# Seven PSUM banks for PE's sums in the third edge pass, and VectorE's additions placed later behind them

## The chip, the cores and the metric

The kernel runs on one core of one Trainium2 chip. The metric is the device time of one execution in microseconds (us). The kernel before took 9835.41 us, the median of three runs that lay between 9833.75 and 9841.89 us. PE is TensorE, DVE is VectorE, ACT is ScalarE, POOL is GpSimd and SP is SyncE, which issues plain DMAs.

## The reference, cut to what matters

Four graph layers follow each other over 6250 nodes and 100000 edges, each with a residual and a layer norm. The second is the one that the change is in. It has two attention heads of 128 columns:

```python
def _gat_head(node_feats, W, a, src, dst, N):
    h = node_feats @ W
    a_l, a_r = (a[0, :C], a[0, C:])
    s_l = h @ a_l
    s_r = h @ a_r
    logits = s_l[src] + s_r[dst]
    e = jnp.exp(-jax.nn.leaky_relu(logits, negative_slope=ALPHA))
    row_sum = jax.ops.segment_sum(e, src, num_segments=N)
    h_prime = jax.ops.segment_sum(e[:, None] * h[dst], src, num_segments=N)
    return jax.nn.elu(h_prime / row_sum[:, None])
```

For each edge, a row of `h` is fetched by `dst`, multiplied by the edge's weight `e`, and added to the sum of its node `src`. `e` itself is one more column, so that a row has 2 x (128 + 1) = 258 columns. No maximum is subtracted in this layer, unlike in the first and the third.

## The kernel before

The edges are sorted by the node whose sum they enter, once by `dst` and once by `src`, and cut into 832 chunks of 128 edges. All edges of a chunk belong to one window of 128 nodes. Six edge passes go over the 832 chunks: a1e and a2e (the two attention layers of the first graph layer), **be** (the layer above), te (dot product attention), and g1e and g2e (plain sums). The first four are `attention_pass`, with `kind` "gat", "gat", "neg" and "dot"; the last two are `sum_pass`. `guarded` is true for "gat" and "dot", so the branches with `not guarded` are of be alone. Between the passes lie dense stages. A pass begins and ends with a barrier of all engines.

A pass is unrolled in 104 steps of eight chunks. Each engine has its own written order, and the engines meet by semaphores alone. In be, with t the step:

- POOL (`gather`) issues eight indirect DMAs a step. Each fetches the 128 rows of a chunk from the table in HBM into a ring of four steps (`RING`). Before the even chunks it waits for DVE's `weigh` of the step four before, which frees the slots.
- SP (`fetch`) loads `place_row`, the place of each edge in its window.
- DVE (`turn`) makes from it the one-hot matrix `turned`, two steps ahead, and PE (`of_node`) multiplies it with `node`, which gives each edge its node's term. DVE adds the three parts of that (`sum_parts`), adds the fetched row's term (`meet`, which first waits until all eight gathers of step t have landed) and applies the leaky slope (`leak`).
- ACT (`weights`) makes the exponentials of a step and (`distances`, `mark`) the one-hot matrix of the next.
- DVE (`weigh`, four times a step, two chunks each, L1239) multiplies the rows with their weights.
- PE (`sums`, eight times a step, L1077) multiplies the one-hot matrix of a chunk with its 258 columns, into a PSUM bank, `ps_u`. Four banks are used in turn.
- DVE (`add`, eight times a step, L1251) adds the bank to the window's part of `acc` in SBUF. The window's number comes from a register, that `Windows` loads for four steps at a time; the first chunk of which it holds a number is the argument `-12`, counted from the step's own.

Semaphores count: `s_summed` PE's sums, `s_added` DVE's additions, `s_summand` the `weigh`s. A sum waits until the addition that empties its bank is done, four chunks before, and an addition waits for its own sum and for the addition before it. In DVE's step t the rows of step t-1 are weighed, the additions 4 to 7 of step t-2 are made, and then the additions 0 to 3 of step t-1.

## Time and profile before

| what | value |
|---|---|
| device time, median of three runs | 9835.41 us |
| device time, lowest and highest | 9833.75, 9841.89 us |
| span of the profiled execution | 11006.2 us |
| pass be in the profiled execution, first gather to last addition | 5247.3 to 6562.2 us |
| DVE, PE and POOL busy in that stretch | 661.5, 721.7 and 812.0 us |
| granted TensorE clock: whole span, that stretch | 0.695, 0.70 |

The profiled execution's own time is known by its span alone, 11006.2 us from the first to the last instruction. It is 1170.8 us, or 12%, above the median of the timed runs, which are executions without the profiler. A number of the trace therefore has to be asked whether it also holds in a timed run. In the rows further down, "idle before" is the time for which an engine did nothing ahead of an instruction, and the name behind it is what ended most of it: "issue" means nothing that the profile shows, "remote" a semaphore whose last event fits no instruction recorded next to it. The shape of an operand is partitions x elements.

### The profile page before, as it was taken

What the parts mean: (1) busy time and instruction counts of PE and PEld (TensorE: products, weight loads), DVE (VectorE), ACT (ScalarE), POOL (GpSimd) and SP (SyncE); (2) the same over time, 40 slices, a digit from 0 to 9 for tenths busy, and PEclk for the clock granted to TensorE, in tenths of its full rate; (3) what the DMA queues carried; (4) which work ended last, traced back from release to release, by engine and by line L of the source; (5) the groups of instructions that cost most, each with busy time, mean ns of one, the idle gap of its engine ahead of it and who ended that gap; (6) DMA issues with size and microseconds to landing.
All of it is one profiled execution on the core that took longest, in us unless ns stands there. A gap on an engine that the chain in (4) does not pass through costs nothing. (4 is left out here: it accounts for less than half of the span.)

```text
span 11006.2 us, 145249 instructions
## 1 busy us (share of the span) xinstructions
PE 6188.8 (56%) x34036; PEld 4327.9 (39%) x34036; DVE 6265.2 (57%) x19166; ACT 4406.9 (40%) x12341; POOL 6558.0 (60%) x6616
## 2 busy tenths in 40 slices
PE   3774577566666444446455557778775343433335
PEld 2443344333343444444233334445554232333334
DVE  7998899566666433335455557999984121211113
ACT  7886788222222222223222223444443233333333
POOL 4996699355554455552566642666655666566663
PEclk6997799766666555556667779999987555555556
DMA  0222122233333212212333343666652111211112
GB/s 21 74 74 67 45 73 73 87 98 99 96 98 82 62 41 41 42 41 45 105 106 107 108 93 123 175 175 175 174 159 64 46 47 45 41 27 23 23 23 35
DMA packets 464040, 862.04 MB, mean 78 GB/s; under 512 B 143184, under 2 KB 204036, under 8 KB 463108
## 3 DMA queue, kind: packets, MB, share of 16 engines
q0 software_dynamic: 226304, 550.69, 20.8%
q1 hardware_dynamic: 236932, 302.17, 9.4%
q8 instruction: 316, 5.18, 0.2%
q14 instruction: 488, 4.00, 0.1%
HBM read 800.28 MB, written 52.14 MB: 77 GB/s over the span
## 5 line engine op out<-in xcount | busy, mean ns | idle before, releaser
L1031 POOL DMA_INDIRECT all_Y<-table,all_row x3328 | 3236.2, 972 | 2394.2 <-DVE all_Y L1239 1243.1
L557 POOL TENSOR_SCALAR all_acc<-all_Y,all_acc 128x128 f16<-128x128 f16 x1176 | 1319.0, 1133 | 229.3 <-DVE all_acc L492 158.9
L1239 DVE TENSOR_TENSOR all_Y<-all_Y 128x512 f32<-128x512 f32 (+1 forms) x1560 | 942.5, 604 | 187.3 <-issue 100.3
L1466 POOL DMA_INDIRECT g2e_rows<-table,all_row x832 | 784.9, 943 | 432.3 <-issue 234.7
L1466 POOL DMA_INDIRECT g1e_rows<-table,all_row x832 | 785.1, 944 | 419.4 <-issue 234.3
L1077 PE MATMUL be_ps_u<-all_Y,be_onehot 128*128 128x258 f32 x1664 | 645.7, 523 | 546.5 <-DVE all_acc L1251 281.8
L1482 PE MATMUL g1e_ps_u<-g1e_rows,g1e_onehot 128*128 128x128 f32 x1664 | 470.3, 426 | 737.0 <-issue 557.9
L1482 PE MATMUL g2e_ps_u<-g2e_rows,g2e_onehot 128*128 128x64 f32 x1664 | 434.8, 431 | 771.9 <-issue 549.5
L1510 DVE TENSOR_TENSOR all_acc<-all_acc,g1e_ps_u 128x128 f32 x832 | 240.0, 288 | 968.0 <-DMA te_place_row<-places_src 594.5
L1077 PE MATMUL a1e_ps_u<-all_Y,a1e_onehot 128*128 128x264 f32 x1664 | 762.3, 589 | 20.1 <-DVE all_acc L1251 11.1
L1510 DVE TENSOR_TENSOR all_acc<-all_acc,g2e_ps_u 128x64 f32 x832 | 184.5, 222 | 1026.1 <-DMA te_place_row<-places_src 624.0
L1482 PEld LDWEIGHTS g2e_ps_u<-g2e_rows,g2e_onehot 128*128 128x128 f32 x1664 | 382.0, 321 | 824.8 <-issue 632.5
L1251 DVE TENSOR_TENSOR all_acc<-all_acc,be_ps_u 128x258 f32 x832 | 350.5, 421 | 606.2 <-remote 385.7
L1482 PEld LDWEIGHTS g1e_ps_u<-g1e_rows,g1e_onehot 128*128 128x128 f32 x1664 | 359.5, 275 | 847.8 <-issue 679.8
L1077 PEld LDWEIGHTS be_ps_u<-all_Y,be_onehot 128*128 128x128 f32 x1664 | 370.7, 253 | 768.5 <-issue 675.4
L495 DVE TENSOR_SCALAR all_acc<-all_Y,all_acc 128x832 f16<-128x832 f16 x1568 | 599.5, 442 | 0.0
L1063 PE MATMUL te_ps_q<-all_X,te_turned 128*128 x1664 | 515.3, 440 | 146.8 <-issue 103.6
L1077 PE MATMUL te_ps_u<-all_Y,te_onehot 128*128 128x264 f32 x1664 | 532.2, 435 | 73.6 <-DVE all_Y L1239 71.5
L1077 PE MATMUL a2e_ps_u<-all_Y,a2e_onehot 128*128 128x66 f32 x1664 | 492.1, 434 | 124.9 <-issue 86.9
L524 ACT ACTIVATE all_Y<-all_Y 128x128 f16<-128x128 f16 x1568 | 476.7, 388 | 96.4 <-PEq L81 96.4
L532 ACT ACTIVATE all_Y<-all_Y,all_acc 128x128 f16<-128x128 f16 x1568 | 477.1, 389 | 3.0 <-DMA all_Y<-codes 3.0
L1077 PEld LDWEIGHTS a2e_ps_u<-all_Y,a2e_onehot 128*128 128x128 f32 x1664 | 397.8, 318 | 145.8 <-issue 121.5
(521 smaller groups left out, 15166.9 us busy)
## 6 DMA issues: line engine op xcount, KB each, us to landing
all_Y<-table,all_row POOLq DMA_INDIRECT x3328
all_Y<-lows SPq DMA_DIRECT2D x196, 256.0 KB
all_Y<-codes SPq DMA_DIRECT2D x196, 256.0 KB
a1e_place_row<-places_dst SPq DMA_DIRECT2D x104, 256.0 KB
a2e_place_row<-places_dst SPq DMA_DIRECT2D x104, 256.0 KB
be_place_row<-places_src SPq DMA_DIRECT2D x104, 256.0 KB
te_place_row<-places_src SPq DMA_DIRECT2D x104, 256.0 KB
te_flags<-flags_src SPq DMA_DIRECT2D x832, 6.0 KB
```

Source lines behind the costliest of these rows:

```text
L495: dve.tensor_scalar(column1[b][:, k, :], lane16, column[b][:, k:k + 1], None, ALU.is_equal).then_inc(s_hot, 1)
L524: act.activation(away[:, k, :], lane16[:, 0:P], ACT.Abs, scale=-1.0, bias=low_t[:, u * 8 + k:u * 8 + k + 1]).then_inc(s_away, 1)
L532: act.activation(unlike[b][:, k, :], code_row[b][:, k * P:(k + 1) * P], ACT.Abs, scale=-1024.0, bias=spaced_t[:, u * 8 + k:u * 8 + k + 1]) ...
L557: pool.tensor_scalar(row1[b][:, k, :], lane16[:, 0:P], row[b][:, k:k + 1], other_t[:, t * 8 + k:t * 8 + k + 1], ALU.is_equal, ALU.mult).th ...
L1031: pool.indirect_dma_start(out=rows[:, r, k, :], out_offset=None, in_=table, in_offset=bass.IndirectOffsetOnAxis(ap=order.row[:, t * 8 + k: ...
L1063: last = pe.matmul(ps_q[pair % 2][:, j * HC:(j + 1) * HC], turned[b][:, k * P:(k + 1) * P], queries[:, bass.ds(windows.at(windows_j, chunk ...
L1077: pe.matmul(ps_u[k % 4][:, 0:R], onehot[b][:, k, :], summand[:, b, k, :], start=True, stop=True).then_inc(s_summed, 1)
L1239: dve.tensor_tensor(out[:, :, :, 0:C], rows[:, r, ks, value_c0:value_c0 + HC].rearrange("p k (h n) -> p k h n", h=H), bc(out[:, :, :, C:C ...
L1251: dve.tensor_tensor(mine, mine, ps_u[k % 4][:, 0:R], ALU.add).then_inc(s_added, 1)
L1466: pool.indirect_dma_start(out=rows[:, r, k, :], out_offset=None, in_=table, in_offset=bass.IndirectOffsetOnAxis(ap=order.row[:, t * 8 + k: ...
L1482: pe.matmul(ps_u[k][:, 0:width], onehot[b][:, k, :], rows[:, r, k, :], start=True, stop=True).then_inc(s_summed, 1)
L1510: dve.tensor_tensor(mine, mine, ps_u[k][:, 0:width], ALU.add).then_inc(s_added, 1)
```

## The change

In be the number of banks goes from four to seven (with the bank of `of_node` these are all eight), and the banks go round by the count of chunks instead of by the chunk's number in its step. A sum then waits for the addition seven chunks before. DVE gets an order of its own for be: its step t makes the additions 2 to 7 of step t-2 and the additions 0 and 1 of step t-1, where it was 4 to 7 and 0 to 3. `sum_parts`, `weigh`, `meet`, `leak` and `turn` are there as often as before; the fourth `weigh` moves ahead of the addition 7 of step t-2. The windows' numbers are loaded from chunk -14 instead of -12, as many as before. The code of the other passes is written in another way, with the same order.

```diff
+    BANKS = 4 if guarded else 7
...
-        ps_u = [m.ps(f"ps_u{b}", [P, 512]) for b in range(4)]
+        ps_u = [m.ps(f"ps_u{b}", [P, 512]) for b in range(BANKS)]
...
-                    wait(pe, s_added, t * 8 + (k - 3))
-                    pe.matmul(ps_u[k % 4][:, 0:R], onehot[b][:, k, :], summand[:, b, k, :], start=True, stop=True).then_inc(s_summed, 1)
+                    wait(pe, s_added, t * 8 + (k + 1 - BANKS))
+                    pe.matmul(ps_u[(t * 8 + k) % BANKS][:, 0:R], onehot[b][:, k, :], summand[:, b, k, :], start=True, stop=True).then_inc(s_summed, 1)
...
-                windows = Windows(nc, order, mybir.EngineType.DVE, -12, U)
+                windows = Windows(nc, order, mybir.EngineType.DVE, -12 if guarded else -14, U)
...
-                    dve.tensor_tensor(mine, mine, ps_u[k % 4][:, 0:R], ALU.add).then_inc(s_added, 1)
+                    dve.tensor_tensor(mine, mine, ps_u[(t * 8 + k) % BANKS][:, 0:R], ALU.add).then_inc(s_added, 1)
...
+                    elif not gat:
+                        sum_parts(t, b)
+                        add(t - 2, 2, -14, j)
+                        weigh(t - 1, n, rp, 0)
+                        add(t - 2, 3, -13, j)
+                        meet(t, b, r)
+                        add(t - 2, 4, -12, j)
+                        weigh(t - 1, n, rp, 1)
+                        leak(t, b)
+                        add(t - 2, 5, -11, j)
+                        weigh(t - 1, n, rp, 2)
+                        add(t - 2, 6, -10, j)
+                        weigh(t - 1, n, rp, 3)
+                        add(t - 2, 7, -9, j)
+                        add(t - 1, 0, -8, j)
+                        turn(t + 2, b)
+                        add(t - 1, 1, -7, j)
+                        return
```

The order on PE, ACT, POOL and SP is the one of before. On DVE the first half of a step of be stands here, of before and of after. `be_spread` is written by `sum_parts`, `all_Y` by `weigh`, `all_acc` by `add` (the row "ISA" ahead of it computes its address and carries the wait for the sum), `be_raw` by `meet` and `be_argument` by `leak`. Before:

```order
L1264 TENSOR_REDUCE be_spread1<-be_ps_n 128x16
L1239 TENSOR_TENSOR all_Y<-all_Y 128x4x128
L1251 ISA
L1251 TENSOR_TENSOR all_acc<-all_acc,be_ps_u0 128x258
L1270 TENSOR_TENSOR be_raw<-be_spread1,all_Y 128x16
L1251 ISA
L1251 TENSOR_TENSOR all_acc<-all_acc,be_ps_u1 128x258
L1239 TENSOR_TENSOR all_Y<-all_Y 128x4x128
L1278 SCALAR_TENSOR_TENSOR be_argument1<-be_raw 128x16
```

After:

```order
L1265 TENSOR_REDUCE be_spread1<-be_ps_n 128x16
L1252 ISA
L1252 TENSOR_TENSOR all_acc<-all_acc,be_ps_u6 128x258
L1240 TENSOR_TENSOR all_Y<-all_Y 128x4x128
L1252 ISA
L1252 TENSOR_TENSOR all_acc<-all_acc,be_ps_u0 128x258
L1271 TENSOR_TENSOR be_raw<-be_spread1,all_Y 128x16
L1252 ISA
L1252 TENSOR_TENSOR all_acc<-all_acc,be_ps_u1 128x258
L1240 TENSOR_TENSOR all_Y<-all_Y 128x4x128
L1279 SCALAR_TENSOR_TENSOR be_argument1<-be_raw 128x16
```

One addition more now stands ahead of the first `weigh` and ahead of `meet`, and each is of a chunk two earlier. The end of the same step, from the third `weigh` on, before:

```order
L1239 TENSOR_TENSOR all_Y<-all_Y 128x4x128
L1251 ISA
L1251 TENSOR_TENSOR all_acc<-all_acc,be_ps_u0 128x258
L1239 TENSOR_TENSOR all_Y<-all_Y 128x4x128
L1251 ISA
L1251 TENSOR_TENSOR all_acc<-all_acc,be_ps_u1 128x258
L1251 ISA
L1251 TENSOR_TENSOR all_acc<-all_acc,be_ps_u2 128x258
L1251 ISA
L1251 TENSOR_TENSOR all_acc<-all_acc,be_ps_u3 128x258
L1229 TENSOR_SCALAR be_turned1<-be_place_row1,all_lane_p 128x1024
```

After:

```order
L1240 TENSOR_TENSOR all_Y<-all_Y 128x4x128
L1252 ISA
L1252 TENSOR_TENSOR all_acc<-all_acc,be_ps_u3 128x258
L1240 TENSOR_TENSOR all_Y<-all_Y 128x4x128
L1252 ISA
L1252 TENSOR_TENSOR all_acc<-all_acc,be_ps_u4 128x258
L1252 ISA
L1252 TENSOR_TENSOR all_acc<-all_acc,be_ps_u5 128x258
L1230 TENSOR_SCALAR be_turned1<-be_place_row1,all_lane_p 128x1024
L1252 ISA
L1252 TENSOR_TENSOR all_acc<-all_acc,be_ps_u6 128x258
```

Before, the first addition behind the third `weigh` is of the sum of this step's first rows; after, it is the addition 6 of the step before, and the first addition of this step's sums stands behind the fourth `weigh` and the addition 7. `turn` is followed by one more addition.

## Rows read from the trace of the kernel before

**Rows 1.** The page's first line.

```profile
span 11006.2 us, 145249 instructions
```

**Rows 2.** Busy time of each engine by pass: a1e, a2e, be, te, g1e, g2e.

```profile
core 0: us, PE busy (x) PEld busy (x) DVE busy (x) ACT busy (x) POOL busy (x), PEclk, DMA share, GB/s
2067.00:3545.00 1478.00, 921.27 (x3906) 575.98 (x3906) 938.04 (x2785) 404.14 (x1239) 836.44 (x832) 0.66 0.38 97
3680.00:5090.00 1410.00, 663.61 (x3952) 569.79 (x3952) 553.08 (x2824) 402.72 (x1248) 792.64 (x832) 0.50 0.24 46
5246.00:6563.00 1317.00, 721.74 (x2496) 442.54 (x2496) 661.53 (x1665) 374.38 (x1040) 812.01 (x832) 0.70 0.40 105
6781.00:8238.00 1457.00, 1123.18 (x4742) 753.29 (x4742) 1316.92 (x2887) 677.68 (x1558) 907.14 (x935) 0.92 0.61 173
8404.00:9618.00 1214.00, 475.44 (x1696) 364.57 (x1696) 245.90 (x842) 367.11 (x942) 785.06 (x832) 0.58 0.20 45
9652.00:10868.00 1216.00, 438.19 (x1681) 384.70 (x1681) 188.61 (x845) 364.08 (x936) 787.88 (x833) 0.50 0.15 23
```

**Rows 3.** The gathers of a1e, a2e, be, g1e, g2e: duration in ns, first and last start.

```profile
L1031 POOL DMA_INDIRECT all_Y<-table,all_row x832: 940/946/1571, 2072.4 to 3525.1; - x167
...
L1031 POOL DMA_INDIRECT all_Y<-table,all_row x832: 938/944/1218, 3683.4 to 5058.9; - x167
...
L1031 POOL DMA_INDIRECT all_Y<-table,all_row x832: 940/946/1464, 5247.3 to 6532.8; - x167
...
L1466 POOL DMA_INDIRECT g1e_rows<-table,all_row x832: 938/944/1045, 8406.6 to 9597.6; - x167
...
L1466 POOL DMA_INDIRECT g2e_rows<-table,all_row x832: 938/944/992, 9656.9 to 10845.9; - x167
```

**Rows 4.** Groups of be by line: busy us, mean ns | idle before, releasers.

```profile
L1031 POOL DMA_INDIRECT all_Y<-table,all_row x832 | 812.0, 976 | 492.6 <-issue 251.6 <-DVE all_Y L1239 223.0 <-POOLq L81 18.0
L1077 PE MATMUL be_ps_u<-all_Y,be_onehot 128*128 128x258 f32 x1664 | 645.7, 523 | 546.5 <-DVE all_acc L1251 281.8 <-issue 263.4
...
L1251 DVE TENSOR_TENSOR all_acc<-all_acc,be_ps_u 128x258 f32 x832 | 350.5, 421 | 606.2 <-remote 385.7 <-PE be_ps_u L1077 115.8 <-issue 75.5
L1239 DVE TENSOR_TENSOR all_Y<-all_Y 128x512 f32<-128x512 f32 x416 | 284.8, 685 | 1.8 <-PE be_ps_u L1077 1.8
```

**Rows 5.** DVE in order of time, be: start us, length us, [idle before].

```profile
5704.39 0.53 DVE L1229 TENSOR_SCALAR be_turned<-be_place_row,all_lane_p 128x1024 bf16<-128x1024 f16 x1
...
5711.36 0.51 DVE L1229 TENSOR_SCALAR be_turned<-be_place_row,all_lane_p 128x1024 bf16<-128x1024 f16 x1
...
5714.79 0.42 DVE L1251 TENSOR_TENSOR all_acc<-all_acc,be_ps_u 128x258 f32 x1 [0.21 <-issue]
5715.13 0.69 DVE L1239 TENSOR_TENSOR all_Y<-all_Y 128x512 f32<-128x512 f32 x1
5724.26 0.42 DVE L1251 TENSOR_TENSOR all_acc<-all_acc,be_ps_u 128x258 f32 x1 [8.44 <-remote]
...
5727.97 0.55 DVE L1229 TENSOR_SCALAR be_turned<-be_place_row,all_lane_p 128x1024 bf16<-128x1024 f16 x1
...
5736.41 0.48 DVE L1229 TENSOR_SCALAR be_turned<-be_place_row,all_lane_p 128x1024 bf16<-128x1024 f16 x1
```

**Rows 6.** PE in order of time, the same stretch.

```profile
5713.25 1.13 PE L1077 MATMUL be_ps_u<-all_Y,be_onehot 128*128 128x258 f32 x4
5714.72 1.31 PE L1077 MATMUL be_ps_u<-all_Y,be_onehot 128*128 128x258 f32 x4 [0.35 <-issue]
5724.83 1.20 PE L1077 MATMUL be_ps_u<-all_Y,be_onehot 128*128 128x258 f32 x2 [8.80 <-issue]
```

**Rows 7.** POOL in order of time, the same stretch.

```profile
5715.28 1.35 POOL L1031 DMA_INDIRECT all_Y<-table,all_row  x1 [0.30 <-issue]
...
5723.19 0.95 POOL L1031 DMA_INDIRECT all_Y<-table,all_row  x1 [0.30 <-issue]
5726.07 0.95 POOL L1031 DMA_INDIRECT all_Y<-table,all_row  x1 [1.93 <-DVE all_Y L1239]
```

More of the change, by code:

```diff
@@ L1381, in step @@
                         return
+                    elif not gat:
[16 more added lines that the diff above has]
+                        return
                     else:
-                        if t == 0 or not gat:
+                        if t == 0:
                             sum_parts(t, b)
@@ L1395, in step @@
                     weigh(t - 1, n, rp, 2)
-                    if guarded:
-                        scan_forward(t, b)
-                        fade_first(t - 1, n, -8, j)
-                        scan_back(t, b)
-                        add(t - 1, 0, -8, j)
-                        weigh(t - 1, n, rp, 3)
-                        row_scan_forward(t, b)
-                        add(t - 1, 1, -7, j)
-                        row_scan_back(t, b)
-                        add(t - 1, 2, -6, j)
-                        drop(t, b)
-                        turn(t + 2, b)
-                        add(t - 1, 3, -5, j)
-                        widen(t, b)
-                        top(t, b)
-                        if gat:
-                            sum_parts(t + 1, n)
-                        subtract(t, b)
-                    else:
-                        add(t - 1, 0, -8, j)
-                        weigh(t - 1, n, rp, 3)
-                        add(t - 1, 1, -7, j)
-                        add(t - 1, 2, -6, j)
-                        add(t - 1, 3, -5, j)
-                        turn(t + 2, b)
+                    scan_forward(t, b)
+                    fade_first(t - 1, n, -8, j)
+                    scan_back(t, b)
+                    add(t - 1, 0, -8, j)
+                    weigh(t - 1, n, rp, 3)
+                    row_scan_forward(t, b)
+                    add(t - 1, 1, -7, j)
+                    row_scan_back(t, b)
+                    add(t - 1, 2, -6, j)
+                    drop(t, b)
+                    turn(t + 2, b)
+                    add(t - 1, 3, -5, j)
+                    widen(t, b)
+                    top(t, b)
+                    sum_parts(t + 1, n)
+                    subtract(t, b)
                 if guarded:
```

## The prediction

> **What bounds the kernel now.** I read the page's first line, then the busy time by pass, then the gathers of each pass, then the groups of be and three engines of it in order of time.
>
> The first line is the oddest: the profiled execution spans 11006.2 us [rows 1], 1170.8 more than the timed median of 9835.4. So the first question is not what be waits for in the trace, but whether a timed run waits for it too.
>
> In be no engine is full: of 1317 us DVE is busy 661.5, PE 721.7 and POOL 812.0 [rows 2]. Three paces can be read.
> - POOL: a gather takes 0.976 us [rows 4], and where nothing holds it the next starts 0.30 us later [rows 7]. That is 1.276 us each and 8 x 1.276 = **10.2 us a step**. 832 of them take 1062 us, but first to last start is 6532.8 - 5247.3 = 1285.5 us [rows 3]. The difference, 224 us, is the wait for DVE's `weigh` to free slots (223.0 us [rows 4]).
> - DVE and PE together: from one `turn` to the next are 6.97 us (5704.39 to 5711.36) and 8.44 us (5727.97 to 5736.41) [rows 5]. Both are below POOL's 10.2.
> - Between these two lies a step of 16.6 us. In it DVE sits idle 8.44 us, put down to "remote" [rows 5], ahead of the addition of a sum that PE's rows show as issued at 5713.25 [rows 6]. PE records four sums until 5716.0, and then nothing for 8.80 us, since the fifth needs DVE's addition. So PE's work is there and its semaphore is late. Such waits sum to 385.7 us [rows 4], as many as 46 of 8.4 us in 104 steps, so nearly every second step has one.
>
> So in the profiled execution be alternates a quick step and one with a silence of PE, and DVE then frees slots too late for POOL. A timed run without the silences would be bound by POOL alone.
>
> **Are the silences in a timed run?** I test it on the whole kernel. If POOL ran at its pace in every pass whose gathers are held up, each would shrink from its first-to-last time to its busy time plus 832 x 0.30 = 249.6 us [rows 2, 3]: a1e from 1452.7 to 1086.0, a2e from 1375.5 to 1042.2, be from 1285.5 to 1061.6, g1e from 1191.0 to 1034.7, g2e from 1189.0 to about 1037. In te, DVE is busy 1316.9 of 1457 us, and I leave it. The differences are 367 + 333 + 224 + 156 + 152 = **1232 us**, against the 1171 us by which the trace is longer than the median. The two agree to 61 us. If the silences were in the timed runs as well, 1171 us would have to be found elsewhere, and te, where DVE is busy 90% of the time, has no room for them. I therefore take it that a timed run has them hardly at all, and that be takes POOL's pace there.
>
> The Trainium skill (page "NOTIFIC — the notification-queue block", section "Interfaces") says of the path by which records leave the engines that its backpressure "is what can stall an engine". That would make the silences the profiler's own. No row here shows that path; by that rule the result is the forecast below, and no number of it rests on it.
>
> **The change part by part.**
> - *Seven banks.* PE's sum waits for the addition seven chunks back. In the trace PE waits 281.8 us for additions [rows 4]. In a timed run at 10.2 us a step, DVE and PE need 7.0 to 8.4, so they have 1.8 to 3.2 us of slack in each step, and the wait is paid out of that. Worth on the end: 0.
> - *DVE's new order.* Eight additions, four `weigh`s, and one each of `sum_parts`, `meet`, `leak` and `turn`, as before. An addition right behind an addition starts 0.63 us after it (0.42 and 0.21 idle), a `weigh` behind an addition 0.34 us [rows 5]. Three pairs of additions stood together in a step, now one: 2 x 0.29 = 0.58 us of DVE a step, 60 us in all. It is covered by POOL's pace, and comes to light only where DVE is the bound.
> - *What is queued behind the waits.* `meet` waits for the landing of step t's gathers. One addition more stands ahead of it, 0.6 us at most, and behind it stand the other `weigh`s of step t-1. These free the slots for the gathers of step t+3, and POOL is then at t+1: two steps, 20 us, of room. Cost 0. `turn` is two steps ahead of its use, and the fourth `weigh` comes 0.3 to 1 us sooner. Cost 0.
> - *The tail.* The last gather starts at 6532.8 [rows 3]. Behind it DVE must still make its part of step 103 and all of 104 and 105. Before that were 7 + 8 + 4 additions, now 6 + 8 + 6: one more, +0.6 us.
> - *Registers and code.* As many window numbers are loaded as before. 0.
> - *What is left of the waits.* The 61 us by which the reconstruction overshoots may be waits that timed runs do have. By its part of 1232 us, be has 61 x 224 / 1232 = 11 us of them. At most all 61 lie in be. If the change removes two fifths of them (91 of 224, as worked out in the first rival), the gain is 4 to 5 us, with bounds 0 and 61.
>
> Sum: +0.6 - 4.5 = -4 us, so the timed median goes from 9835 to **9831 us**. I make it against the timed median, since the profiled span holds the silences. In the profiled execution itself the change may show more: be could lose up to 224 us of its 1317 there.
>
> **The rivals.**
> 1. *The silences are in the timed runs too, and be is bound by DVE and PE* (faster). Then DVE's order counts. The 60 us of separated additions come through. Under each silence DVE makes one `weigh` more before it blocks, since the first addition of the new sums now stands behind the fourth `weigh`: 0.6 us in each of 52 pairs of steps, 31 us. Together 91 us: 9835 - 91 = **9744 us**. Bounds: 0 (the silence grows by what DVE works ahead) and POOL's pace, 224 us: 9611 us. For it: 385.7 us of DVE's idle time and 223.0 of POOL's in be. Against it: the sum of 1232 against 1171.
> 2. *The gathers grow longer* (slower). A gather takes 976 ns in be and 785.06 / 832 = 944 ns in g1e, where DVE has no `weigh` [rows 2, 4]; the gather at 5715.28, beside a `weigh` at 5715.13, took 1.35 us [rows 5, 7]. So the `weigh`s cost POOL some 32 x 832 = 27 us. If the new order puts twice as many beside gathers, POOL, the bound, pays 27 us more: **9862 us**. It decides from a mean gather of 1000 ns on (24 x 832 = 20 us). Against it: neither the number of `weigh`s nor their length changes.
>    The Trainium skill ("SBUF — State Buffer", section "Who interferes with whom") says that a VectorE instruction with two SBUF inputs contends with a GpSimd instruction that reads SBUF. The 1.35 us fits it. The rule speaks against any change that moves `weigh`s onto gathers; it gives no price here.
> 3. *PE is not set free.* The sum 7 of a step still needs the addition 0 of the same step, at the end of DVE's step, so that PE stays tied to DVE. That too gives no change: 9835 us. I count it with the forecast.
>
> **How the numbers follow.** A measurement of this kernel tells 0.2%, about 20 us, from no change. The forecast, with rival 3, has 0.64. Faster has 0.29: most of it is rival 1, and the rest is the case that most of the 61 us lie in be and go. Slower has 0.07, rival 2. The low end of the range takes in rival 1 at its own price and leaves the stretch from 9740 down to 9611 (about 0.08) out. The high end takes in rival 2. So 9740 to 9860; the forecast's own range is 9815 to 9850.
>
> **What would show each step right or wrong.** In the profile of the changed kernel I expect fewer waits of PE for additions (281.8 before), one pair of additions side by side in a step instead of three, and a quick step of about 6.4 instead of 7.0 us, while a step's eight gathers stay at 10.2 us. The silences should still be there, since nothing in the change touches their cause, and be may shorten in the profile without the timed median moving. That split is the sign of the forecast. The mean gather should stay at 976 ns. The prediction is wrong if the timed median falls by more than 20 us: then be is bound by DVE and PE in timed runs as well, and the step that failed is the test on the whole kernel, with the 1171 us lying elsewhere than in the waits of POOL.

## The result: slower by 22 us, and the profile after

The changed kernel takes 9858.01 us (median of 14 runs, 9850.68 to 9863.64), the kernel before 9835.76 us in as many runs beside it (9828.03 to 9846.62). The ratio is 1.002, with an interval of 1.0013 to 1.0027. So the change costs 22 us where -4 was forecast. The time lies in the range, the sign was given a chance of 0.07, and what made it slower is none of the rivals as they were written.

**Two levels.** One thing has to be known before the numbers can be compared: one and the same program takes some 9830 us in some measurements and some 11020 to 11130 us in others, with or without a profile, and runs that are compared stand beside each other at one level. I call them the lower and the upper level. The profile of the kernel before (11006.2 us, [rows 1]) is an execution at the upper one, the profile of the changed kernel one at the lower. No profile of the kernel before fell at the lower level. Nearest to it there is the run r14_banks_only further down, the kernel before with seven banks, at 1.0004 of its time.

The page's first line, the busy time of be (columns as in [rows 2]) and the gathers of a1e, a2e, be, g1e and g2e (as [rows 3]), of the changed kernel:

```profile
span 9857.9 us, 145246 instructions
```

```profile
4575.00:5710.00 1135.00, 679.95 (x2496) 498.74 (x2496) 659.74 (x1674) 375.80 (x1042) 837.38 (x832) 0.73 0.48 122
```

```profile
L1032 POOL DMA_INDIRECT all_Y<-table,all_row x832: 942/946/1454, 2077.3 to 3186.9; - x167
...
L1032 POOL DMA_INDIRECT all_Y<-table,all_row x832: 940/944/1254, 3336.4 to 4393.3; - x167
...
L1032 POOL DMA_INDIRECT all_Y<-table,all_row x832: 942/946/1475, 4582.2 to 5671.7; - x167
...
L1476 POOL DMA_INDIRECT g1e_rows<-table,all_row x832: 940/944/1045, 7559.6 to 8597.0; - x167
L1476 POOL DMA_INDIRECT g2e_rows<-table,all_row x832: 940/944/992, 8660.7 to 9698.0; - x167
```

The groups of be by line (as [rows 4]):

```profile
L1032 POOL DMA_INDIRECT all_Y<-table,all_row x832 | 837.4, 1006 | 272.5 <-issue 238.8 <-POOLq L81 19.4 <-DVE all_Y L1240 14.3
...
L1078 PE MATMUL be_ps_u<-all_Y,be_onehot 128*128 128x258 f32 x1664 | 611.7, 533 | 268.9 <-DVE all_Y L1240 267.0 <-DVE all_acc L1252 1.8
...
L1252 DVE TENSOR_TENSOR all_acc<-all_acc,be_ps_u 128x258 f32 x832 | 348.7, 419 | 43.2 <-DVE all_acc L1252 16.6 <-PE be_ps_u L1078 8.9 <-issue 7.8
L1240 DVE TENSOR_TENSOR all_Y<-all_Y 128x512 f32<-128x512 f32 x416 | 285.0, 685 | 0.0
```

What the reader is to see: DVE's 385.7 us of silences ("remote", [rows 4]) are gone, and nearly all of POOL's 223.0 us of waits for `weigh` (14.3 are left). POOL idles 272.5 us for 832 gathers, 0.33 each. It is the bound of be, with hardly a hole. PE no longer waits for additions (1.8 us). All this is the level and not the change: r14_banks_only, which has DVE's old order and lies at the lower level, shows the same (POOL waits 19.5 us for `weigh`). But the gathers take 837.4 us instead of 812.0, 1006 ns each instead of 976.

There is one thing more, which no group of be shows, since a register load isn't counted as busy. These are the loads of window numbers (`Windows`, L888) in be: duration in ns (least, median, most), first and last start. Here are DVE's in the kernel before, and then PE's own and DVE's in the changed kernel:

```profile
L888 DVEq TENSOR_LOAD <-all_window x27: 2098/2102/2109, 5264.8 to 6551.1; - x27
```

```profile
L888 PEldq TENSOR_LOAD <-all_window x27: 2127/2134/2152, 4581.6 to 5637.5; - x27
L888 DVEq TENSOR_LOAD <-all_window x27: 7125/7137/7175, 4599.8 to 5689.7; - x27
```

As many numbers are loaded, 27 times 32, but each of DVE's loads takes 7.14 us instead of 2.10. That is 27 x 5.03 = 136 us of DVE's time. In DVE's own order of time one such load looks like this (the idle time in brackets; the load itself has no row):

```profile
5637.91 0.40 DVE L1252 TENSOR_TENSOR all_acc<-all_acc,be_ps_u 128x258 f32 x1
5644.78 0.21 DVE L1265 TENSOR_REDUCE be_spread<-be_ps_n 128x16 f32<-128x48 f32 x1 [6.47 <-issue]
5645.35 0.42 DVE L1252 TENSOR_TENSOR all_acc<-all_acc,be_ps_u 128x258 f32 x1 [0.36 <-issue]
5645.69 0.69 DVE L1240 TENSOR_TENSOR all_Y<-all_Y 128x512 f32<-128x512 f32 x1
5646.29 0.42 DVE L1252 TENSOR_TENSOR all_acc<-all_acc,be_ps_u 128x258 f32 x1
5646.62 0.18 DVE L1271 TENSOR_TENSOR be_raw<-be_spread,all_Y 128x16 f32<-128x16 f32 x1
```

### The profile page after: what moved, and what is told of

It reads as the page before. It is cut to its first block and busy times, and to the rows that moved or that the text cites. A ratio compares the mean times of both kernels' runs of the same rounds, so it can differ in the third digit from the quotient of the medians.

```text
span 9857.9 us, 145246 instructions
## 1 busy us (share of the span) xinstructions
PE 6075.9 (62%) x34036; PEld 4356.6 (44%) x34036; DVE 6264.1 (64%) x19166; ACT 4401.9 (45%) x12341; POOL 6604.6 (67%) x6616
## 5 line engine op out<-in xcount | busy, mean ns | idle before, releaser
L1032 POOL DMA_INDIRECT all_Y<-table,all_row x3328 | 3284.8, 987 | 1497.4 <-issue 1036.6
L1492 PE MATMUL g1e_ps_u<-g1e_rows,g1e_onehot 128*128 128x128 f32 x1664 | 428.7, 439 | 630.8 <-issue 313.7
L1492 PE MATMUL g2e_ps_u<-g2e_rows,g2e_onehot 128*128 128x64 f32 x1664 | 406.5, 426 | 652.3 <-DMA g2e_rows<-table,all_row 327.3
L1078 PE MATMUL be_ps_u<-all_Y,be_onehot 128*128 128x258 f32 x1664 | 611.7, 533 | 268.9 <-DVE all_Y L1240 267.0
L1078 PEld LDWEIGHTS be_ps_u<-all_Y,be_onehot 128*128 128x128 f32 x1664 | 430.8, 272 | 403.5 <-DVE all_Y L1240 312.9
L1064 PEld LDWEIGHTS te_ps_q<-all_X,te_turned 128*128 128x128 f32 x1664 | 320.0, 207 | 299.2 <-issue 258.9
```

Source lines behind the costliest of these rows:

```text
L1032: pool.indirect_dma_start(out=rows[:, r, k, :], out_offset=None, in_=table, in_offset=bass.IndirectOffsetOnAxis(ap=order.row[:, t * 8 + k: ...
L1064: last = pe.matmul(ps_q[pair % 2][:, j * HC:(j + 1) * HC], turned[b][:, k * P:(k + 1) * P], queries[:, bass.ds(windows.at(windows_j, chunk ...
L1078: pe.matmul(ps_u[(t * 8 + k) % BANKS][:, 0:R], onehot[b][:, k, :], summand[:, b, k, :], start=True, stop=True).then_inc(s_summed, 1)
L1492: pe.matmul(ps_u[k][:, 0:width], onehot[b][:, k, :], rows[:, r, k, :], start=True, stop=True).then_inc(s_summed, 1)
```

## The experiments

The first twelve runs test what I first held to be open: whether banks, order or the second SBUF input of `weigh` count. Ten of them fell at the upper level, where the changed kernel itself never ran. r13_after and r14_banks_only repeat two of them at the lower level. r15 to r17 test the load, and r18_after_again is the changed kernel once more. Ratios are this kernel over the kernel before on the same chip, with the 95% interval.

**Both kernels again.** The kernel before once more:

> The kernel before, unchanged, once more with a profile, since the profiled execution shown first spans 11006 us against a timed 9836. Theory A (be is bound by POOL's gathers in a timed run, and the change made them longer): the span is about 9835 us, POOL in be hardly waits for VectorE (under 40 us), the 832 gathers take about 1065 us from first to last start, with a mean near 976 ns, some 30 ns under the 1006 ns of the changed kernel. Theory B (the 22 us come from somewhere else): the mean gather in be is within 5 ns of 1006.

Measured: 11010.6 us, beside 11019.59 as the median of timed runs without a profile. The same once more, on another chip:

> The kernel before, unchanged, with a profile. If this chip is at the lower level (about 9830 us): theory A (the gathers of be, which are the bound, got longer) wants a mean gather in be some 25 to 30 ns under the 1006 ns of the changed kernel, first to last gather about 1065 us against 1090, and the other passes alike within 5 us. Theory B wants the same length of be, and the 20 us in another pass.

Measured: 11157.82 us beside 11130.49. So the timed runs have the upper level as well, and neither run fell at the level that its theories were written for. The changed kernel, three times:

> The changed kernel, unchanged, beside the kernel before on the same chip. The kernel before has shown two levels that have nothing to do with its code: 9836 us, and 11006 to 11020 us with long silences of PE's semaphores. Theory A1: at the upper level be waits on VectorE and PE, and the new order, which lets VectorE weigh two chunks more under a silence, shortens be by up to 91 us (about 10930 beside 11020); at the lower level it is 22 us longer (9858 beside 9836). Theory A2: at the upper level too the new order lengthens be, since VectorE's order is now tied to PE one step later; the run with five banks and the new order was 237 us longer there.

> The changed kernel unchanged. Chips have shown two levels for the same program (9825 to 9836, or 11019 to 11130 us for the kernel before), and the changed kernel has been timed on the lower alone. At the upper level: if VectorE's new order is what made the runs with five banks and weights from PSUM 222 to 252 us longer, this is about 11240, with 220 us more in be; if the five banks or the weights in PSUM were, it is 11020 or less. At the lower level: ratio 1.002, mean gather in be 1006 ns.

> The changed kernel unchanged, once more, for a chip at the upper level. There, with VectorE and PE the bound in be, its loads of 7.13 us put 27 x 5.03 = 136 us more on VectorE's path, less what the new order saves: ratio 1.005 to 1.02. At the lower level: 1.0018 to 1.0020, as three times before.

Measured: 9843.43 against 9825.05 us, 1.0018 (1.0008 to 1.0027); 9847.16 against 9827.51, 1.0018 (1.0009 to 1.0028); 9856.66 against 9834.86, 1.0019 (1.001 to 1.0028). be's gathers stretch over 1090.6, 1090.5 and 1092.5 us from the first one's start to the last one's end, 1090.5 in the profile above, and each of the 27 loads took 7.13 us in all three. The loss is real, and the slow load with it. The chip is not what sets the level: the same one gave the upper level in r1_before_again and the lower in r18_after_again.

**Seven banks alone, in the old order.** DVE's order and the start of its windows stay as before:

```diff
+    BANKS = 4 if guarded else 7
...
-        ps_u = [m.ps(f"ps_u{b}", [P, 512]) for b in range(4)]
+        ps_u = [m.ps(f"ps_u{b}", [P, 512]) for b in range(BANKS)]
...
-                    wait(pe, s_added, t * 8 + (k - 3))
-                    pe.matmul(ps_u[k % 4][:, 0:R], onehot[b][:, k, :], summand[:, b, k, :], start=True, stop=True).then_inc(s_summed, 1)
+                    wait(pe, s_added, t * 8 + (k + 1 - BANKS))
+                    pe.matmul(ps_u[(t * 8 + k) % BANKS][:, 0:R], onehot[b][:, k, :], summand[:, b, k, :], start=True, stop=True).then_inc(s_summed, 1)
...
-                    dve.tensor_tensor(mine, mine, ps_u[k % 4][:, 0:R], ALU.add).then_inc(s_added, 1)
+                    dve.tensor_tensor(mine, mine, ps_u[(t * 8 + k) % BANKS][:, 0:R], ALU.add).then_inc(s_added, 1)
```

> The kernel before with the seven banks and the bank counting of the change, but VectorE's old order. Theory A (the weighings of the new order fall on gathers more often): VectorE's order is to blame and not the banks, so this is the time of before, 9836 us within 5, gathers in be as long as before. Theory B (PE, freed by more banks, slows the gathers or the landing by its own accesses): the 22 us appear here, about 9858 us.

> Seven banks with VectorE's old order, again, since the first run of it was at the upper level, where POOL is not the bound. At the lower level theory A wants the time of before (ratio 1.000) and its mean gather; theory B, that PE's freer running costs the 20 us, wants a ratio of 1.002.

> Seven banks with VectorE's old order, for the lower level (about 9830 us for the kernel before); both runs of it so far fell on chips at the upper level. At the lower level theory A (the new order puts weighings on gathers) wants the time of before, ratio 1.000 within 0.001, and a mean gather in be near 980 ns, against 1006 ns in the changed kernel. Theory B (PE's freer running costs the 20 us) wants 1.002 and 1006 ns. At the upper level: 1.001 to 1.004 as twice before.

> Seven banks with VectorE's old order. At the lower level theory A (the new order puts weighings on gathers) wants the time of before, ratio 1.000 within 0.001, and a mean gather in be near 980 ns against 1006; theory B (PE's freer running costs the 20 us) wants 1.002 and 1006 ns. At the upper level: 1.001 to 1.004, as three times before.

Measured at the upper level: 11039.4 against 11019.59 us, 1.0013 (1.0001 to 1.0024); 11168.31 against 11130.49, 1.0036 (1.0023 to 1.0049); 11032.58 against 11019.29, 1.0014 (1.0005 to 1.0023). At the lower: 9832.45 against 9827.51, 1.0004 (0.9995 to 1.0014). Seven banks gain nothing at either level, and lose a little at the upper one. The lower run stood beside r13_after on one chip, and there the whole change costs 1.0018. So the loss lies in the order or in what came with it. Its span, its gathers, its group of gathers and its loads:

```profile
span 9838.7 us, 145246 instructions
```

```profile
L1032 POOL DMA_INDIRECT all_Y<-table,all_row x832: 942/946/1466, 4581.5 to 5664.9; - x167
```

```profile
L1032 POOL DMA_INDIRECT all_Y<-table,all_row x832 | 831.2, 999 | 272.3 <-issue 233.6 <-DVE all_Y L1240 19.5 <-POOLq L81 19.2
```

```profile
L888 DVEq TENSOR_LOAD <-all_window x27: 2098/2103/2118, 4598.8 to 5681.8; - x27
```

The old order at the lower level has gathers of 999 ns. This is the figure that the 1006 of the changed kernel must be held against, not the 976 of the upper level: where POOL waits less, more of its gathers meet a `weigh` (452 here, 391 in the trace of before). Against this run r13_after's gathers take 6 us more in all, and its last addition ends 6 us later behind the last gather (32.9 and 27.1 us). That is 12 of the 15 us between the two medians.

**Five banks instead of seven in the changed kernel** (`BANKS = 4 if guarded else 5`):

> The changed kernel with five banks in place of seven, nothing else. At the lower level (9836 for the kernel before) POOL is the bound and five banks are enough: 9858, as the changed kernel. At the upper level (11020): if the 237 us of the run with the weights in PSUM and five banks came from the banks, this is about 11256; if they came from VectorE's order, the changed kernel itself is that long, and this too; if they came from the weights in PSUM, this is at 11020 or under it.

Measured: 9846.3 against 9825.05 us, 1.002 (1.0011 to 1.003), with the changed kernel itself at 1.0018 on that chip. In the new order at the lower level it doesn't matter whether there are five banks or seven.

**`weigh` reads its factors from PSUM.** ACT writes `exp` a second time, into two PSUM banks, and `weigh` takes its factors there, so that it has one SBUF input instead of two. The changed kernel has five banks here, to make room:

```diff
+    NWEIGHT = 1 if dot else 2
...
+                ps_w = [m.ps(f"ps_w{b}", [P, 512]) for b in range(2)]
...
+        def factor(b):
+            return ps_w[b][:, 0:8 * H].rearrange("p (h k) -> p h k", h=H)
...
+                        act.activation(factor(b), argument[b][:, 0, :, :], ACT.Exp, scale=-1.0).then_inc(s_weight, 1)
...
-                        dve.wait_ge(s_weight, (t + 1) * NARG)
+                        dve.wait_ge(s_weight, (t + 1) * NWEIGHT)
...
+                    by = out[:, :, :, C:C + 1] if guarded else factor(b).rearrange("p h (k n) -> p k h n", n=1)[:, ks, :, :]
...
-                                      bc(out[:, :, :, C:C + 1], [P, 2, H, C]), ALU.mult).then_inc(s_summand, 1)
+                                      bc(by, [P, 2, H, C]), ALU.mult).then_inc(s_summand, 1)
```

In the kernel before:

> The kernel before, where ScalarE writes be's weights a second time into PSUM (one activation more a step) and VectorE's weighing reads the weight from there, so that it has one input in SBUF in place of two. Theory A (a weighing with two SBUF inputs holds up the gather beside it): mean gather in be falls from about 976 to about 945 to 950 ns, and the time falls by 22 to 27 us to about 9811 us. Theory B (the gathers are slowed by something else, or not at all by the weighing's inputs): mean gather and time as before, 9836 us or a little more.

> The kernel before with the weights of be read from PSUM, again, for the lower level. At the upper level the mean gather in be fell from 974 to 952 ns. Theory A wants that here too, and now in the time: 832 x 22 ns = 18 to 20 us under the kernel before, ratio 0.998. Theory B: ratio 1.000.

In the changed kernel:

> The changed kernel with the same weights from PSUM; the two banks for them are taken from the sums, which have five in place of seven. Theory A: mean gather in be falls from 1006 to about 945 to 950 ns, the order of VectorE no longer matters, and the time is that of the kernel before with weights from PSUM, about 9811 us, 47 below the changed kernel. Theory B: about 9858 us, as the changed kernel.

> The changed kernel with the weights from PSUM and five banks, again, for the lower level, where five banks alone left the changed kernel as it was (ratio 1.002 and 1.0018). Theory A: mean gather in be falls from 1006 to about 952 ns, 832 x 54 = 45 us, so that the ratio to before is about 0.998, the same as that of the kernel before with weights from PSUM. Theory B: ratio 1.002.

> The changed kernel with the weights of be read from PSUM and five banks, for the lower level. Theory A: mean gather in be about 952 ns in place of 1006, so that 832 x 54 = 45 us go and the time is about 9803 where the kernel before takes 9830, ratio 0.997. Theory B: ratio 1.002. At the upper level: 1.021 to 1.022 as twice before.

All five fell at the upper level. In the kernel before: 11015.21 against 11019.59 us, 1.0004 (0.9992 to 1.0015), and 11150.76 against 11130.49, 1.0016 (1.0005 to 1.0028). In the changed kernel: 11256.37 us, 1.0209 (1.0193 to 1.0226); 11382.96, 1.0222 (1.0208 to 1.0236); 11241.03 against 11019.29, 1.0202 (1.0188 to 1.0216). These are the range and the group of the gathers in the kernel before with the edit (r3_before_weight_in_psum), and then the group, the range and the loads in the changed one (r4_after_weight_in_psum). The stretch of the second row takes in the first 16 gathers of te as well:

```profile
L1037 POOL DMA_INDIRECT all_Y<-table,all_row x832: 940/946/1192, 5245.9 to 6527.8; - x167
```

```profile
L1037 POOL DMA_INDIRECT all_Y<-table,all_row x848 | 807.7, 952 | 539.7 <-issue 286.4 <-DVE all_Y L1248 232.9 <-POOLq L81 20.3
```

```profile
L1038 POOL DMA_INDIRECT all_Y<-table,all_row x832 | 791.7, 952 | 734.9 <-DVE all_Y L1249 481.5 <-issue 235.1 <-POOLq L81 18.2
```

```profile
L1038 POOL DMA_INDIRECT all_Y<-table,all_row x832: 940/946/1269, 5256.0 to 6763.5; - x167
L888 DVEq TENSOR_LOAD <-all_window x27: 7122/7126/7146, 5273.3 to 6781.2; - x27
```

Two things follow. The gathers do become short, 952 instead of 976 ns, and at this level nothing comes of it, since POOL waits for DVE. And the new order together with five banks, these factors and the slow loads is some 2% slower there: be grows from 1281.9 to 1507.5 us, and POOL waits 481.5 us for `weigh`, against 232.9 in the kernel before with the same edit. What had grown of DVE's own work were the loads alone. 27 x 5.03 = 136 us is the larger part of these 226 us. But DVE's waits put down to "remote" grew too, from 412.6 us to 521.1 us, 108 us more. That the slow loads are the cause of both is argued, not shown: no run without the slow load fell at this level, and the new order and the five banks are rivals that stay untested here.

**Where the slow load comes from.** A load takes 32 numbers of four bytes from `order.window`, from `t0 * 8 + (first + LEAD)` on. The change moves DVE's `first` from -12 to -14, since an addition may now belong to an earlier step. With this the load starts 8 bytes past a multiple of 16, counted from the start of `order.window`; with -12, and in PE's own loads, it starts at such a multiple. I call the first an odd start and the second an even one. Two theories: the start is the cause (A), or the place of the load in the new order is (B). `Windows` was given a count and a period of its own, so that the same numbers can be had from an even start. In the changed kernel, starting at -16:

```diff
+        self.count = count or U * 8
...
-            self.order.window[0:1, bass.ds(t0 * 8 + (self.first + LEAD), self.U * 8)], engines=(self.engine_type,), min_val=0, max_val=NW - 1,
+            self.order.window[0:1, bass.ds(t0 * 8 + (self.first + LEAD), self.count)], engines=(self.engine_type,), min_val=0, max_val=NW - 1,
...
-        return self.values[j * 8 + chunk - self.first]
+        return self.values[j % self.U * 8 + chunk - self.first]
...
-                if windows is not None and t % U == 0:
+                if windows is not None and t % windows.U == 0:
...
-                windows = Windows(nc, order, mybir.EngineType.DVE, -12 if guarded else -14, U)
+                windows = Windows(nc, order, mybir.EngineType.DVE, -12, U) if guarded else Windows(nc, order, mybir.EngineType.DVE, -16, 2, 20)
```

> The changed kernel, with its banks and VectorE's order, but VectorE's window numbers in be are loaded for two steps at a time, 20 of them from chunk -16 on (a start of 0 instead of 8 bytes within 16), in place of 32 from chunk -14. In the changed kernel each of the 27 loads took 7.13 us, and 2.10 us in the kernel before (from -12, 16 bytes on). Theory L (the load's start is what costs): a load takes about 20/32 x 2.10 = 1.3 us; at the lower level (9827 for the kernel before) the tail of be is 5 us shorter and the gathers regain the rest, ratio to before 1.000 to 1.001 in place of 1.0018; at the upper level (11020) be falls to the time of before or under it. Theory O (the order itself costs, the load is hidden by the 2 us of slack in each step): ratio 1.002 at the lower level.

and in the kernel before the opposite, the same edit with `-14, 2, 20`, whose start is 8 bytes off:

> The kernel before, with its four banks and its order, but VectorE's window numbers in be are loaded for two steps at a time, 20 of them from chunk -14 on, the start of the changed kernel's loads. Theory L: each of 53 loads takes 20/32 x 7.13 = 4.5 us, so VectorE has 53 x 4.5 - 27 x 2.1 = 180 us more in be; at the lower level the last load lengthens the tail by 2 to 3 us and the gathers somewhat, ratio 1.001; at the upper level be is 100 to 180 us longer, ratio 1.01 to 1.016. Theory O: loads of about 1.3 us and a ratio of 1.000 at both levels.

Both ran on one chip at the lower level. Measured: the changed kernel with the even start 9814.94 against 9823.17 us, **0.9992** (0.9983 to 1.0001); the kernel before with the odd one 9840.82, **1.0017** (1.0008 to 1.0026). Span, loads, gathers and their group, first of the changed kernel with the even start:

```profile
span 9816.8 us, 145272 instructions
```

```profile
L889 DVEq TENSOR_LOAD <-all_window x53: 1346/1351/1370, 4589.2 to 5657.5; - x53
```

```profile
L1033 POOL DMA_INDIRECT all_Y<-table,all_row x832: 942/946/1470, 4571.9 to 5640.6; - x167
```

```profile
L1033 POOL DMA_INDIRECT all_Y<-table,all_row x832 | 816.5, 981 | 272.0 <-issue 239.7 <-POOLq L81 18.8 <-DVE all_Y L1241 13.4
```

then of the kernel before with the odd one:

```profile
L889 DVEq TENSOR_LOAD <-all_window x53: 4482/4496/4523, 4591.4 to 5682.7; - x53
```

```profile
L1032 POOL DMA_INDIRECT all_Y<-table,all_row x832: 942/946/1415, 4574.2 to 5665.8; - x167
```

```profile
L1032 POOL DMA_INDIRECT all_Y<-table,all_row x832 | 839.5, 1009 | 271.0 <-issue 244.6 <-POOLq L81 17.8 <-DVE all_Y L1240 8.5
```

Twenty numbers take 1.35 us from an even start and 4.50 from an odd one, and 32 take 2.10 and 7.13: 66 to 68 ns a number against 223 to 225. Theory B falls, since the old order with the odd start has the slow load and the new order with the even start hasn't. The price follows the load: taking it out brings the ratio from 1.0018 or 1.002 to 0.9992, some 26 us, and putting it into the kernel before costs 17. Both kernels have 53 loads of 20 numbers, so more and shorter loads are not what separates them. But they differ in DVE's order, and no run has the old order with 53 quick loads or the new one with 27 quick ones. So what the shorter loads are worth by themselves is not measured, and the 26 and the 17 both hold it. An estimate, if neither piece depends on the order: the start costs (26 + 17) / 2 = some 21 us, and the shorter loads give back 4 or 5.

**How an engine that isn't the bound makes the bound longer.** In all lower-level runs POOL's idle time stays at 271 to 273 us. What differs is the length of its gathers: 816.5 us with the quick load, 837.4 with the slow one, 21 us. The rest is the tail. This is its end in DVE's order of time in the changed kernel; the last load, which starts at 5689.7, stands behind the last gather, where POOL no longer covers it:

```profile
5689.70 0.42 DVE L1252 TENSOR_TENSOR all_acc<-all_acc,be_ps_u 128x258 f32 x1 [0.21 <-PE be_ps_u L1078]
5697.07 0.42 DVE L1252 TENSOR_TENSOR all_acc<-all_acc,be_ps_u 128x258 f32 x1 [6.95 <-issue]
...
5706.52 0.42 DVE L1252 TENSOR_TENSOR all_acc<-all_acc,be_ps_u 128x258 f32 x1 [0.21 <-DVE all_acc L1252]
```

From the last gather's end to the last addition are 32.9 us in r13_after and 27.4 in r15_after_aligned_load: 5 us. 21 and 5 are the 26 us. In the old order the same two pieces are smaller. From r14_banks_only (seven banks, 27 quick loads) to r16_before_misaligned_load (four banks, 53 slow ones) the gathers grow by 8 us (831.2 to 839.5) and the tail by 2 (27.1 to 29.3).

Why the gathers grow was read from the trace. Sorted by how long before them a load of DVE's started, their number and mean length are (in r14_banks_only and the changed kernel a load comes every fourth step, in the other two every second):

```
                             0 to 5 us     5 to 10 us    10 to 15 us   15 to 20 us
changed kernel               104, 945 ns   104, 1072     101,  996      96, 1009
r14_banks_only (old order)   102, 1001     102, 1004     104,  964      96, 1041
r15_after_aligned_load       205, 947      206, 1008     198,  965     194, 1009
r16_before_misaligned_load   208, 959      202, 1128     201,  948     183, 1005
```

While DVE makes a slow load, the gathers take their undisturbed 945 ns. Behind it DVE catches up, additions and `weigh`s side by side as in the rows from 5644.78 on, and the gathers beside them take 1072 and 1128 ns instead of 1004 to 1008. For the kernel with the odd start that is 37 of the 54 us by which its gathers exceed 944 ns. But this is not the price of the load: with the old order and quick loads (r14_banks_only) the excess is 46 us already. The slow load mostly moves the disturbance to one place, and adds little to its sum in this order. In the changed kernel that place holds 13 of 52 us, and the others are longer too: 314 gathers beside one `weigh` take 1009 ns, where the even start has 312 of 963 ns. There `weigh`s are no more often beside gathers, but each costs more; that it depends on where within the gather a `weigh` falls I take for likely, and no run tells.

**Even start and factors from PSUM together** (the edits of r15_after_aligned_load and of the PSUM runs, five banks):

> The changed kernel with the aligned loads of the run r15, and with be's weights read from PSUM (two banks for them, five for the sums). Theory A (a weighing with two inputs in SBUF holds up a gather beside it): at the lower level (9823 for the kernel before) the mean gather in be falls from 981 ns in r15 to about 950, 832 x 31 = 26 us, so about 9790 us, ratio 0.9965. If the gathers are lengthened by something else, 0.9992 as r15. At the upper level the same kernel with the 7.13 us loads was 2.0 to 2.2% slower than before: if the loads did that (27 x 5 = 136 us of VectorE and what it draws with it), this is at 1.01 or under; if the order did, still at 1.02.

Measured, at the lower level: 9799.18 against 9834.86 us, **0.9963** (0.9949 to 0.9977). This beats both kernels. Span, gathers, their group and that of `weigh`:

```profile
span 9795.1 us, 145378 instructions
```

```profile
L1039 POOL DMA_INDIRECT all_Y<-table,all_row x832: 942/947/1184, 4578.6 to 5620.5; - x167
```

```profile
L1039 POOL DMA_INDIRECT all_Y<-table,all_row x832 | 789.6, 949 | 272.6 <-issue 227.1 <-DVE all_Y L1250 26.2 <-POOLq L81 19.4
...
L1250 DVE TENSOR_TENSOR all_Y<-all_Y,be_ps_w 128x512 f32<-128x512 f32 x416 | 282.7, 680 | 0.1
```

`weigh`s are as long (680 against 685 ns) and run beside 443 gathers, against 408 in r15_after_aligned_load, yet only 7 gathers take over 1000 ns, where there it is 171. So nearly all of the gathers' excess is `weigh`'s second SBUF input. The rule of the Trainium skill ("SBUF — State Buffer", "Who interferes with whom"), that a VectorE instruction with two SBUF inputs contends with a GpSimd instruction that reads SBUF, is borne out here: 816.5 - 789.6 = 27 us of 832 gathers. The page gives no such price.

## Why the prediction was wrong, point by point

- **Registers and code: "As many window numbers are loaded as before. 0."** This is the step that failed. The count is right, the length isn't: 7.13 us instead of 2.10, for the start of a load has a price. The rows of the loads in the trace of before (2.10 us, start at -12) would have given the length of one, and the -14 stood in the diff; but every load in that trace has an even start, so its price could not have been read there. No bound was put on it, in a sum where other unknowns had one. Held against r15_after_aligned_load the term is +26 us at the lower level: 21 of gathers and 5 of tail. The estimate from both pairs of runs, with the shorter loads taken out, is some 21.
- **The silences, and POOL as the bound.** The reconstruction was right. At the lower level be's gathers stretch over 1089.5 us, g1e's over 1037.4, g2e's over 1037.3, a1e's over 1109.6 and a2e's over 1056.9, where it gave 1062, 1035, 1037, 1086 and 1042. be, a1e and a2e are off by 28, 24 and 15 us. In be and a1e most of that is the gathers' length, which I took from the upper level, where fewer meet a DVE instruction: 812.0 there and 837.4 here in be, 836.4 and 857.4 in a1e. In a2e it is 4 us of the 15. In be the slow load is in the 28 as well: the old order has 1083.4. te, which was left out, is as long at both levels (1451.3 and 1459.0 us). What was wrong is the reason: the 1171 us are not the profiler's. The timed runs beside r1_before_again have them without a profile. The sentence of the Trainium skill on the page "NOTIFIC — the notification-queue block" carried no number, and the timed runs do not bear it out here. What I called a trace that differs from the timed runs was an execution at the other level. The count was wrong too: the 385.7 us are 77 waits of 5.0 us in the mean, as the row below shows, and not some 46 of 8.4. One half of the sign that the forecast named, a be that is shorter in the profile, did appear (1314.9 us from the first gather to the last addition before, 1124.8 after). But it is the level that made it: r14_banks_only, in the old order, has 1111.4. The mean gather, for which 976 ns was named, is read the same way: 999 in the old order, 1006 in the changed kernel.

```profile
  remote: 385.7, 77
```

- **Seven banks: 0.** Right at the lower level (1.0004; five banks as seven).
- **DVE's new order.** Forecast 0 on the path, with 60 us of DVE covered. By r15_after_aligned_load the change without the slow load goes at 0.9992, -8 us, with -17 to +1 as its interval: the forecast of -4 fits, and so does none at all. Its gathers take 816.5 us where the old order with seven banks has 831.2. The number and length of the loads differ between these two as well. For the order speaks that it decides how many gathers meet a `weigh`, whatever the loads: some 450 in the old one (r14_banks_only and r16_before_misaligned_load), 401 and 408 in the new one (the changed kernel and r15_after_aligned_load).
- **Waits, `meet`, `turn`: 0.** POOL waits 14.3 us for `weigh` in the changed kernel and 19.5 in r14_banks_only. Right.
- **The tail: +0.6 us.** 27.4 us with the quick load against 27.1 in r14_banks_only. Right, but for the slow load.
- **What is left of the waits: -4.5 us.** At the lower level there are none left to gain. The -8 us came through shorter gathers, so the size fits by chance.
- **Rival 1** (9744 us) is what the upper level would have to show. The only runs of the new order there, with the slow load, five banks and factors in PSUM, went the other way, by 2%. Whether the order gains at that level without the load stays open.
- **Rival 2** (9862 us) came nearest to the time of 9858, and its bound was met, 1006 ns. But its cause was to be the new order, and with a quick load this order has 981 ns. Its price of `weigh`'s second input, 27 us, was measured at 27. That the figures are the same is luck in part: the 27 was read at the upper level in the old order, and the gathers' excess over 944 ns at the lower level is 46 us in the old order and 31 in the new one with quick loads. The measured time lies inside the range because its high end was put there for this rival: that, too, is luck.

## What to carry to other kernels

Where an edit shifts the index at which a load of register values starts, look at the loads' own rows: their length isn't counted as busy time, and at 8 bytes past a multiple of 16 they took 3.3 to 3.4 times as long. An engine with slack can still cost the bound, through what it does beside it when it catches up. And before a trace is read for what bounds a stage, its span must be held against the timed runs: here 12% between them meant another bound, POOL in the one and DVE with PE in the other.

## What the runs showed of the hardware

- A register load of n numbers took 66 to 68 ns a number from a start at a multiple of 16 bytes, and 223 to 225 from 8 bytes past one (20 and 32 numbers). The loads of 16 numbers in te, which start at such a multiple too, took 1.10 us, 69 ns a number. Other offsets weren't tried, and why it is so is open. The Trainium skill ("Runtime: NRT & Kernel Launch", "Instruction fetch mechanics") says that a register load takes some 200 ns a register even for bulk; it speaks of loads from HBM, and these are from SBUF. The odd start is near that figure, the even one is a third of it, and for loads like these the measurement decides.
- A gather of 128 rows takes 0.945 us and is followed by 0.30 us of idle time; beside two `weigh`s with both inputs in SBUF its mean was 1216 ns in the changed kernel (86 gathers).
- The program has two levels 12 to 13% apart (9823 to 9836 and 11019 to 11130 us for the kernel before). At the upper one DVE waits 77 times in be, 385.7 us in all and up to 10.7 us each, for what the profile puts down to "remote". In the stretch of [rows 5] and [rows 6] PE's rows have the awaited sum as issued at 5713.25, and its addition starts at 5724.26; whether the sum itself or its semaphore is late, the trace doesn't tell. What makes the level is open; it is neither the profiler nor the chip as such.
